# A two-layer gated attention and expert kernel: k projected into the second staging bank, late maxima turned behind it, and ranks, v, the context turn and the shared expert moved by one or two heads

## What is computed

```python
x = x + tanh(g_xattn[0]) * L0_xattn(layernorm(x), ctx, ctx, Wq, Wk, Wv, bv, Wo, bo)  # causal mask, 16 heads of 16
x = x + tanh(g_ffn[0])   * L0_ffn(layernorm(x), ...)    # softmax gate, top 2 of 8 experts (silu) + a shared expert
x = x + tanh(g_xattn[1]) * L1_xattn(layernorm(x), ctx, ctx, mask, Wq, Wk, Wv, Wo)    # key mask by length
x = x + tanh(g_ffn[1])   * L1_ffn(layernorm(x), ...)    # cosine gate, top 2 of 8 experts (gelu, 1024 wide)
```

## Time and profile before

| | us |
|---|---|
| three runs | 1715.0, 1718.82, 1719.96 (median 1718.82) |
| profiled execution: its time | 1725.34 |
| its span, first to last instruction | 1723.3 |
| layer 0's steps, the ten from 137.15 to 420.02 | 282.87 |
| layer 1's steps, the ten from 897.40 to 1179.72 | 282.32 |
| TensorE busy / VectorE / ScalarE / GpSimd | 1376.0 / 1075.0 / 797.8 / 732.2 |

### The profile page before, as it was taken

How to read it: one execution, slowest core, us unless ns; L and a number is a source line. 1 busy time by engine, 2 the same in 40 slices (tenths; PEclk the granted TensorE clock), 3 DMA queues, 4 the chain that set the end, 5 groups by cost and what they waited for, 6 DMA issues and landing times. The chain is left out here.

```text
span 1723.3 us, 39989 instructions
## 1 busy us (share of the span) xinstructions
PE 1376.0 (80%) x12001; PEld 1174.9 (68%) x12002; DVE 1075.0 (62%) x3573; ACT 797.8 (46%) x1760; POOL 732.2 (42%) x694
## 2 busy tenths in 40 slices
PE   3798889888872777735888888888727999999997
PEld 3577777767651766734565566565417999999997
DVE  4587768786753455433788787877645555555543
ACT  2364545554430555531555455555513454444543
POOL 4334444443231566644335454543233334545522
PEclk9999999999985999965999999999968999999999
DMA  2434333433217577642333333332263423434422
GB/s 89 108 97 122 85 108 101 126 79 97 57 56 226 104 130 116 108 89 69 100 101 102 109 95 110 100 105 73 68 178 106 99 48 87 97 86 98 95 40 43
DMA packets 213628, 168.25 MB, mean 98 GB/s; under 512 B 21462, under 2 KB 207096, under 8 KB 213240
## 3 DMA queue, kind: packets, MB, share of 16 engines
q1 hardware_dynamic: 181112, 126.05, 26.6%
q0 software_dynamic: 26880, 35.80, 12.1%
q10 hardware_dynamic: 5504, 4.75, 1.0%
HBM read 63.80 MB, written 51.56 MB: 67 GB/s over the span
## 5 line engine op out<-in xcount | busy, mean ns | idle before, releaser
L1811 POOL DMA_INDIRECT out_rows<-e_y,e_token x68 | 110.3, 1622 | 235.7 <-DVE e_y L1867 215.9
L1893 ACT ACTIVATE e_h<-e_h,t_up_bias 128x256 f32<-128x256 f32 x272 | 110.6, 444 | 209.1 <-PE e_h L1929 209.1
L773 POOL DMA_INDIRECT routed_rows_dram<-r_rows,r_slot x128 | 127.3, 995 | 187.3 <-DVE r_rows L1043 104.7
L941 DVE TENSOR_REDUCE a_row_max<-a_scores 128x2 f32<-128x512 f32 x256 | 171.6, 680 | 48.7 <-PE a_scores L1584 48.5
L1272 ACT ACTIVATE s_w_rows<-a_scores_t 128x384 f32<-128x384 f32 (+1 forms) x256 | 134.8, 547 | 107.2 <-PE a_scores_t L1602 64.1
L1272 ACT ACTIVATE a_probs<-a_scores_t 128x384 f32<-128x384 f32 (+1 forms) x256 | 135.9, 544 | 100.1 <-PE a_scores_t L1602 51.1
L1944 PE MATMUL e_y_bank<-e_down_hi,e_hidden_hi 128*128 128x256 f32 x544 | 157.8, 290 | 3.1 <-DVE e_hidden_lo L1840 3.1
L1929 PE MATMUL e_h<-e_xs_hi,e_up_hi 128*128 128x256 f32 x544 | 154.8, 285 | 3.7 <-DVE e_xs_lo L1832 3.5
L2102 POOL DMA_INDIRECT x_mid_dram<-l_y,l_token x76 | 119.8, 1577 | 83.8 <-ACT l_token L2196 46.1
L1929 PE MATMUL e_h<-e_xs_lo,e_up_hi 128*128 128x256 f32 x544 | 154.0, 283 | 0.0
L1944 PE MATMUL e_y_bank<-s_k_stack,e_hidden_hi 128*128 128x256 f32 x544 | 153.8, 283 | 0.0
(11 more groups left out here) (287 smaller groups left out, 4326.8 us busy)
## 6 DMA issues: line engine op xcount, KB each, us to landing
s_q_stack<-a_parts SPq DMA_DIRECT2D x384, 64.0 KB
s_k_stack<-a_parts SPq DMA_DIRECT2D x384, 64.0 KB
l_xs_rows<-routed_rows_dram SPq DMA_DIRECT2D x42, 258.0 KB
e_xs_rows<-routed_rows_dram SPq DMA_DIRECT2D x36, 258.0 KB
a_ctx_rows<-in_ctx SPq DMA_DIRECT2D x32, 256.0 KB, 3.2
t_up<-in_L_ffn_W SPq DMA_DIRECT2D x8, 1024.0 KB
t_down<-in_L_ffn_W SPq DMA_DIRECT2D x8, 1024.0 KB
routed_rows_dram<-pad_rows ACTq DMA_DIRECT2D x16, 258.0 KB, 10.0
```

What stands on the lines that cost most here:

```text
L773: pool.indirect_dma_start(out=xs, out_offset=bass.IndirectOffsetOnAxis(ap=slot[p][:, k, c:c + 1], axis=0), in_=rows[p][:, k, c, :], in_off ...
L941: nc.vector.reduce_max(row_max[:, :, h], bank[:].rearrange("p (c t) -> p c t", c=TC), AX_X).then_inc(maxed, 1)
L1811: pool.indirect_dma_start(out=x_acc, out_offset=bass.IndirectOffsetOnAxis(ap=token[p][:, c:c + 1], axis=0), in_=y[p][:, c, :], in_offset=N ...
L1893: nc.scalar.activation(out, h_bank[g][:, at:at + TS], act_func, bias=routed.up_bias[:, bass.ds(e * FC + fc, 1)]).then_inc(hidden_ready, 1)
```

## The change

The k projection goes to `stage[1]` and no longer waits for q to be copied; the late maxima are turned into `stage[0]`, behind it. The shared expert's second half moves from head 15 to head 6, with VectorE's two operations for it (`bend_hidden` from head 12 to head 4, `add_shared` from the step's end to head 7). v moves from head 11 to 13 in layer 0 and to 12 in layer 1, the context turn of layer 0 from 13 to 14, the ranks of layer 1 from 9 to 8, the turn of the normalized rows from 13 to 14, and ScalarE's copy of the early maxima from 13 to 12. The waits that guard the banks follow.

```diff
-        GATE_AT, O_AT, V_AT, RANK_AT, CTX_AT = (1 if soft else 2, 4, 11, 9, 13)
-        MARK_AT = 5 if soft else 8
+        GATE_AT, O_AT, V_AT, RANK_AT, CTX_AT = (1, 4, 13, 9, 14) if soft else (2, 4, 12, 8, 13)
+        MARK_AT = 5 if soft else 6
+        DOWN_AT = 6
@@ vector, step
+                    if h == DOWN_AT - 2 and soft and i.has(-2):
+                        bend_hidden(i)
+                    if h == DOWN_AT + 1 and soft and i.has(-2):
+                        add_shared(i)
-                    if h == 12 and soft and i.has(-2):
-                        bend_hidden(i)
-                if soft and i.has(-2):
-                    add_shared(i)
@@ scalar, step
                 if i.has(2):
                     evac_q(i)
+                if causal and i.has(2):
+                    evac_k(i)
                 if i.has(0):
                     stack_max(i, 0, 1)
-                if causal and i.has(2):
-                    evac_k(i)
-                    if h == 13 and i.has(1):
+                    if h == 12 and i.has(1):
                         stack_max(i, 1, 0)
-                    if h == 13 and i.has(-1):
+                    if h == 14 and i.has(-1):
                         evac_route(i)
@@ tensor
-                turned = stage[half][0:MP * HH, 0:S // 2].bitcast(BF16)
+                turned = stage[0][0:MP * HH, 0:S // 2].bitcast(BF16)
@@ project_k
-                pe.wait_ge(q_ready, b + 1)
-                project_t(stage[0], 1, ctx_t[p], k_done)
+                project_t(stage[1], 1, ctx_t[p], k_done)
@@ gate_rows_of
-                need(pe, max_t_ready, 2 * i.upto(0))
+                if i.has(2):
+                    need(pe, k_ready, i.upto(2))
@@ rank
+                if soft:
+                    need(pe, sh_added, b + 1)
@@ shared_down
-                need(pe, ctx_t_ready, i.upto(3))
-                need(pe, counted, b + 1)
+                if i.has(-1):
+                    need(pe, x_updated, i.upto(-1))
@@ tensor, step
-                if i.has(0):
-                    turn_max_late(i)
                 if i.has(2):
                     project_k(i)
+                if i.has(0):
+                    turn_max_late(i)
```

More of the change, by code:

```diff
@@ L1481, in gate_rows_of @@
                 need(pe, r_xn_t_ready, b + 1)
-                need(pe, max_t_ready, 2 * i.upto(0))
-                if soft:
-                    need(pe, sh_added, b)
+                if i.has(2):
+                    need(pe, k_ready, i.upto(2))
+                elif i.has(0):
+                    need(pe, v_ready, i.upto(0))
                 else:
                     need(pe, counted, b)
-                    need(pe, k_ready, i.upto(2))
+                if not soft and i.has(0):
+                    need(pe, max_t_ready, 2 * i.upto(0))
                 for c in range(TC):
@@ L1502, in project_heads @@
             def project_heads(i):
-                need(pe, max_t_ready, 2 * i.upto(0))
-                need(pe, gate_copied, i.upto(-2))
+                if i.has(-2):
+                    need(pe, gate_copied, i.upto(-2))
+                elif i.has(2):
+                    need(pe, k_ready, i.upto(2))
                 pe.wait_ge(heads_t_ready, i.at(-1) * 2 + 2)
@@ L1512, in project_v @@
             def project_v(i):
-                need(pe, ctx_t_ready, i.upto(2))
-                need(pe, max_t_ready, 2 * i.upto(0))
-                need(pe, x_updated, i.at(0))
-                need(pe, counted, i.upto(-2))
+                need(pe, ctx_t_ready, i.at(1) + 1)
+                if i.has(-2):
+                    need(pe, counted, i.upto(-2))
+                elif i.has(-1):
+                    need(pe, x_updated, i.upto(-1))
+                elif i.has(2):
+                    need(pe, k_ready, i.upto(2))
                 project(stage[1], 2, ctx_t[i.par(1)], v_done)
@@ L1536, in turn_xn @@
                 pe.wait_ge(xn_ready, b + 1)
-                need(pe, k_ready, i.upto(2))
-                need(pe, sh_bent if soft else gate_copied, i.upto(-2))
+                if i.has(-2):
+                    need(pe, sh_bent if soft else gate_copied, i.upto(-2))
+                elif i.has(0):
+                    need(pe, max_t_ready, 2 * i.upto(0))
+                elif i.has(2):
+                    need(pe, q_ready, i.upto(2))
                 turn(stage[0], lambda c, kc: xn[p][:, c, kc * P:kc * P + P], xn_turned)
@@ L1543, in turn_ctx @@
                 pe.wait_ge(ctx_loaded[p], (i.half(3) + 1) * 16)
-                need(pe, counted, i.upto(-2))
-                need(pe, v_ready, i.upto(1))
-                need(pe, x_updated, i.at(0))
+                if i.has(1):
+                    need(pe, v_ready, i.upto(1))
+                elif i.has(2):
+                    need(pe, k_ready, i.upto(2))
                 turn(stage[1], lambda c, kc: ctx_rows[p][:, c, kc * P:kc * P + P], ctx_turned)
             def turn_max_early(i):
-                need(pe, xn_t_ready, i.upto(3))
+                if i.has(3):
+                    need(pe, xn_t_ready, i.upto(3))
+                else:
+                    need(pe, sh_bent if soft else gate_copied, i.upto(-2))
                 turn_max(i, 1, 0)
@@ L1646, in step @@
                         project_heads(i)
-                    if h == V_AT and i.has(1):
-                        project_v(i)
+                    if h == DOWN_AT and soft and i.has(-2):
+                        shared_down(i)
                     if h == 8 and i.has(3):
@@ L1652, in step @@
                         rank(i)
+                    if h == V_AT and i.has(1):
+                        project_v(i)
                     if h == CTX_AT and i.has(3):
@@ L1656, in step @@
                         turn_max_early(i)
-                    if h == 13 and i.has(-1):
+                    if h == 14 and i.has(-1):
                         turn_route(i)
-                    if h == 15 and soft and i.has(-2):
-                        shared_down(i)
             pipeline(pe, step, B, FIRST, LAST, HEAD, TAIL)
```

45 lines of the change are left out of this document (26 added, 19 removed).

## The result

The changed kernel took 1737.82 us (median of four runs, 1730.17 to 1747.62) against 1718.57 for the kernel before: a ratio of 1.0133, 95% interval 1.0098 to 1.0168. It is slower; 1681 was forecast. (A ratio here is the record's, taken over all runs; it can lie up to 0.2% from the quotient of the two medians.) The profiled execution took 1747.62, at the upper end of its four runs.

The account below looks back on a forecast made before the run. TensorE was taken as the bound, VectorE close behind. Gains of 1.2 and 1.7 us per step of layers 0 and 1, thirteen steps each, made 38 us: 1687 from the profiled 1725.3, stated as 1681; eight-in-ten range 1653 to 1712.

Parts of the forecast that it names:

- The step that failed: TensorE's v: moved later, it no longer waits for `counted`, gaining 1.11 us per step of layer 0, 1.2 of layer 1.
- The sum by TensorE: TensorE's waits removed less new waits added: -1.5 us per step of layer 0, -1.8 of layer 1.
- The two new waits: TensorE ahead of the context turn, 1.3 us in layer 0 and about 1.0 in layer 1; at `project_q`, 0.5 more.
- the clock's price: TensorE's lower clock after a long stand: 1.6 us charged per such step, half of the 3.15 seen in one step.
- The slower rival: The gate waits for `k_ready` through the whole hold, TensorE standing over 2 us every step: 12 us slower, 1731; chance 0.11.
- the hold: TensorE's signals arrive late, 2.50 us (layer 1: 2.30) after GpSimd's last scatter starts; read as going with the scatters.
- The floor by VectorE's loop: VectorE's loop through scatters, hold and next maxima limits a step to 26.7 us in layer 0, 26.4 in layer 1.
- the two sums of the prediction: TensorE's waits and VectorE's loop, worked out separately: -1.5 and -1.6 us per step in layer 0, -1.8 both in layer 1.
- The charge for `add_shared` in the loop: VectorE, layer 0: `add_shared`, 0.75 us, moves from outside into the loop and lengthens it.
- that of the turned rows: TensorE's turned rows waiting for the copy of the early maxima: 0.94 us per step goes.
- The ranks' wait: TensorE, layer 1: ranks waiting for the chosen experts, 16.4 us over 16 waits; 0.5 a step taken as gain.
- k's wait: TensorE's k waiting for q's copy, 14 times, 20.7 us in all; its removal forecast to gain 0.65 per step.

Follow-up runs that it names:

- `before_again`: The kernel before, unchanged, run again for its trace beside the experiments: 1688.18 us, ratio 1.0009.
- `after_again`: The changed kernel, unchanged, run again beside the experiments: 1715.03 us, ratio 1.0157 to the kernel before.
- `heads_early`: The changed kernel with VectorE's transposition of the first half of the heads one head earlier: 1681.39 us, ratio 0.9987 to the kernel before.
- `only_k`: The kernel before with k's part alone: k into the second bank without q's copy, late maxima behind it in the first: 1681.57 us, ratio 1.0000.
- `only_down`: The kernel before with the shared expert's second half at head 6 in layer 0, VectorE's two operations at heads 4 and 7: 1674.43 us, ratio 0.9948.
- `v_back`: The changed kernel with v back at head 11 and the context turn at 13 in layer 0: 1671.97 us, ratio 0.9903 to the kernel before.
- `best_v11`: `v_back` with k and the late maxima of layer 1 as in the kernel before: 1658.54 us, ratio 0.9843 to the kernel before.
- in 1: Experiment 1, the kernel before with one part of the change at a time: v's part ratio 1.0227, k's 1.0000, the shared expert's 0.9948.

## Why the prediction was wrong

**The step that failed** is "v two heads later in layer 0, one in layer 1: `counted` is then long given, and 1.11 per step goes". The wait for the count went, but the text did not ask what v's wait and v's own 1.7 us had covered. Next on TensorE behind v stands the group of head 13, which needs VectorE's transposition, and VectorE comes to that only behind the rows and the maxima of head 11. 1.85 came in the place of 1.11. The order of the programs showed this group ahead of the moved v, with `a0_heads_turned` among its waits; the prediction read only that it stood there.

**The sum by TensorE** was right in its form. For layer 0 a step is its busy time and its waits: for `before_again` 24.35 + 1.11 + 0.94 + 0.59 = 26.99 (measured 27.07), for `after_again` 26.01 + 1.85 + 1.16 + 0.38 = 29.40 (29.30), for `heads_early` 24.69 + 0.17 + 1.16 + 0.38 = 26.40 (26.40). The two new waits that it named were sized well for layer 0: 1.16 ahead of the context turn where 1.3 stood, 0.38 at `project_q` where 0.5 stood. The one that it lacked makes the waits 3.39 instead of 2.64, which is 0.75 of the loss of 2.23 per step.

**The rest is busy time, and most of that the clock.** 26.01 less 24.35 is 1.66 more busy time for the same work. About 0.5 of it is there at the full clock too: 24.7 in `heads_early` and in the full-clock steps of the changed kernel, 24.2 in those of before; what brings it stays open. The other 1.1 or so goes with the granted clock. Six of the ten steps in the record's layer 0 have 0.89. In both traces of the changed kernel every stretch of slow matmuls in these steps has a stand of 1.85 ahead of it; not every stand of 1.85 has such a stretch behind it (28.06 at 1.00 above), and in `heads_early`, whose longest stand is 1.16, none of ten steps has one. A long stand is not needed for a single fall: one of the ten steps of `before_again` has 0.95, with no stand above 1.11 in it. The prediction put the clock's price at 1.6 for a step with a long stand and used it only in a rival. The Trainium skill ("TensorE: Matmul & The Clock Gate", What's actually happening) says that the array is throttled unless activity lifts it, and these rows agree.

**The slower rival** (0.11, 1731) came near in its number and was wrong in its place: it had the stand ahead of the gate, from k's signal in the hold. In the trace after, which has the hold, TensorE waits for k there in no step of the twenty, and `only_k`, without the hold, has ratio 1.0000. What layer 1 does have in that trace is a stand of 1.3 to 1.9 just ahead of the gate, for exponentials that stand behind the held copy of the late maxima; but those steps are as long as before's (28.30 against 28.23), and layer 0, where the loss is, has none. That the number came near was luck.

**The floor by VectorE's loop**, 26.7 in layer 0 and 26.4 in layer 1, is no floor of the kernel. Without the hold steps of 25.67 and 26.17 were measured, with the same instructions on VectorE; under the hold, from which it was worked out, no run came near enough to test it. That the two sums of the prediction agreed was chance, and lent them a certainty that neither had. The charge for `add_shared` in the loop doesn't show in `only_down`, where the steps grew shorter by 1.0, again without the hold.

**Layer 1** was forecast at -1.8 per step; beside each other the kernels show -0.46 (27.32 to 26.86), and the whole of it is busy time: the waits of 0.1 us and more rose from 3.2 to 3.7 a step. The wait for the count fell from 1.38 to 0.35, as forecast, and that of the turned rows went. But the mixed group waits for VectorE's transposition here as well, 0.5 in nine of the ten steps, a second term that the sum lacked; the context turn waits 0.3 where 1.0 stood, and `project_q` 0.44 where 0.5 stood. The ranks' wait grew from 0.56 to 1.26 instead of shrinking by 0.5: they were moved a head earlier themselves, and by my reading TensorE comes to them sooner by more than the choice does; it wasn't tried apart. And k's part makes the step 0.5 to 0.6 longer there (26.85 in `v_back`, 26.25 in `best_v11`), with 0.61 of waits of the transposed scores for exponentials that the traces without the hold show only with it. By the rows of `only_k` in 1 they come through the copy of the late maxima, which ScalarE reaches later; no run takes that apart. The clock had a part of its own: before has 0.94 in all ten of its steps, the changed kernel 1.00 in nine, and PE's busy time fell by 1.0 with it.

**k's wait**, 20.7 us in the first trace, was the hold's: in `before_again` the wait of that line comes to 4.2 in 6 places, all short. The gain charged to it, 0.65 a step, was not there to be had in general.

## What to carry to other kernels

Where a job is moved out of a place in which it waits, list what stands next behind it on its engine and when each of their own waits would be given: the old job and its wait were their cover. A wait shortened on one side of an in-order engine is worth only the difference to the next one. And price a longer stand of TensorE twice, as idle time and as the slower matmuls that may follow it. Where a step gets shorter, look which column it came from: in layer 1 the moves exchanged waits for waits of about the same sum, and the gain came with the granted clock.

## What the runs showed of the hardware

The hold is not a property of the program. In the traces of the two kernels that gave the result TensorE's signals reached ScalarE and VectorE up to 2 us and more late, about 2.0 to 2.5 us after the start of the fourth scatter; in the traces of the same kernels taken later on another chip, with the same scatters in the same places, a copy began 0.04 us behind the modelled end of its matmuls, as in every trace of the experiments on three chips, and the kernel before took 1.8% less. The 50 to 100 ns that the Trainium skill ("Advanced Engine Details and Errata", Miscellaneous Facts) gives for the reading of a semaphore are of the order of that trace's 0.04 and far from the first's 2 us. Whether the chip, other traffic or something else makes the difference stays open; no experiment tried it.

The granted clock is sensitive to little: in `only_k` steps of layer 1 with the same jobs alternate between 1.00 and 0.94, 26.54 and 28.04 us, through all ten. And the kernel before has 0.94 in each of its ten there, with a longest wait of 1.38 in them, while the changed kernel has 1.00 in nine of ten (`after_again`), with a longest wait of 1.26 and more waiting in sum.
